# A four-layer block in fp32: the feed-forward's feature reads issued ahead of the following writes, and its normalisation in two halves

## What is computed

```python
x = x + attention_a(layernorm(x))
x = x + ffn(layernorm(x))
x = x + gla(layernorm(x))
x = x + ffn(layernorm(x))
# ffn, with gate_w, up_w [1024, 256], down_w [256, 1024] cubic splines through ~2033 control points each
gate, up = h @ gate_w.T, h @ up_w.T
return (silu(gate) * up) @ down_w.T
```

## Time and profile before

| | us |
|---|---|
| median of 3 runs (lowest, highest) | 847.05 (846.56, 850.43) |
| the profiled execution, its own time | 852.93 |
| span of that execution | 851.2 |

### The profile page before, as it was taken

One profiled execution on the slowest core, in us unless ns is written; L12 is line 12 of the kernel. 1 busy time (PEld: TensorE's weight loads), 2 busy tenths in 40 slices (PEclk: granted clock), 3 DMA queues, 4 the chain that ended last, 5 costly groups with the idle time before them and its releaser, 6 DMA issues.

```text
span 851.2 us, 19705 instructions
## 1 busy us (share of the span) xinstructions
PE 776.4 (91%) x6676; PEld 657.4 (77%) x6676; DVE 629.5 (74%) x1272; ACT 494.8 (58%) x967; POOL 237.0 (28%) x306
## 2 busy tenths in 40 slices
PE   3689999999999999977999989999998879999988
PEld 3567767777777777746988889888888758889887
DVE  7464777777777788836778777789989748887765
ACT  3135545455454555655666657588878746666653
POOL 2942222223232223321000010055656552000000
PEclk9767999999999999977999999999999989999999
DMA  5946566666666654577565651000034125777741
GB/s 183 112 69 88 94 124 100 88 88 88 98 98 94 96 80 78 109 248 262 204 230 218 255 204 45 1 2 2 2 111 168 42 79 202 255 259 272 267 159 50
DMA packets 70960, 111.16 MB, mean 131 GB/s; under 512 B 7061, under 2 KB 27958, under 8 KB 70854
## 3 DMA queue, kind: packets, MB, share of 16 engines
q1 hardware_dynamic: 70896, 110.35, 51.0%
HBM read 41.82 MB, written 42.81 MB: 99 GB/s over the span
## 4 chain that ended last, share of the span: by engine, by line
PE 51%; DVE 14%; issue 9%; DMA 8%; SPq 8%; ACT 6%; POOL 3%; ACTq 0%; DVEq 0%; POOLq 0%
PE bank L414 8%; PE bank L415 6%; PE bank L416 6%; DMA stk<-fx 5%; PE pair_a L878 4%; SPq L586 4%; PE bank L892 4%; PE pair_b L847 4%; DVE inter L1874 3%; DMA fx<-fs 3%; PE pair_a L1166 2%; ACT gact L1457 2%; DVE spline L1952 2%; PE bank L1201 2%; DVE spline L1961 1%
## 5 line engine op out<-in xcount | busy, mean ns | idle before, releaser
L414 PE MATMUL bank<-wd_hi,in_hi 128*128 128x256 f32 x512 | 145.5, 284 | 1.4 <-DVE in_lo L1879 0.9
L416 PE MATMUL bank<-wd_hi,in_lo 128*128 128x256 f32 x512 | 144.9, 283 | 0.0
L415 PE MATMUL bank<-wd_lo,in_hi 128*128 128x256 f32 x512 | 144.5, 282 | 0.0
L668 POOL TENSOR_SCALAR_AFFINE_SELECT prob<-prob 128x512 f32<-128x512 f32 x128 | 82.1, 642 | 217.3 <-ACT prob L1322 217.3
L1322 ACT ACTIVATE prob<-pair_a 128x768 f32<-128x768 f32 x128 | 103.7, 810 | 66.5 <-PE pair_a L878 65.5
L1465 ACT ACTIVATE in_hi<-inter 128x512 fp32r<-128x512 f32 x128 | 80.8, 631 | 105.7 <-DVE inter L1874 100.6
L1703 DVE TENSOR_REDUCE mx<-pair_b 128x6 f32<-128x768 f32 x124 | 118.0, 952 | 26.2 <-PE pair_b L859 25.3
L1879 DVE TENSOR_TENSOR in_lo<-inter,in_hi 128x512 fp32r<-128x512 f32 x128 | 89.1, 696 | 60.5 <-ACT in_hi L1465 59.0
L414 PEld LDWEIGHTS bank<-wd_hi,in_hi 128*128 128x128 f32 x512 | 96.7, 189 | 6.9 <-DVE in_lo L1879 1.7
L415 PEld LDWEIGHTS bank<-wd_lo,in_hi 128*128 128x128 f32 x512 | 96.5, 188 | 4.6
L416 PEld LDWEIGHTS bank<-wd_hi,in_lo 128*128 128x128 f32 x512 | 96.5, 189 | 0.0
(11 more groups left out here) (226 smaller groups left out, 1953.1 us busy)
## 6 DMA issues: line engine op xcount, KB each, us to landing
stk<-fx SPq DMA_DIRECT2D x128, 252.0 KB
stack<-stage SPq DMA_DIRECT2D x192, 128.0 KB, 4.7
fx<-fs SPq DMA_DIRECT2D x32, 512.0 KB, 3.4
fx<-fs SPq DMA_DIRECT2D x32, 256.0 KB, 3.6
fx<-fs SPq DMA_DIRECT2D x16, 504.0 KB
fx<-fs SPq DMA_DIRECT2D x16, 252.0 KB
X<-in_attn_a_x SPq DMA_DIRECT2D x14, 256.0 KB, 5.1
result<-X SPq DMA_DIRECT2D x7, 512.0 KB, 7.9
```

The source lines that it names most:

```text
L414: pe.matmul(dst, l_hi, r_hi, start=first, stop=False)
L415: pe.matmul(dst, l_hi, r_lo, start=False, stop=False)
L416: return pe.matmul(dst, l_lo, r_hi, start=False, stop=last)
L668: pool.affine_select(out=diag, in_=diag, compare_op=ALU.is_ge, fill=0.0, base=0, pattern=[[0, 2], [0, 2], [1, P]], channel_multiplier=-1). ...
```

## The change

Three edits, all in the feed-forward, with the same computation: `read(g+1)` goes ahead of `write_x(g+2)` in SyncE's period; its wait for group g's first up product becomes one for the last up product of group g-1, with a wait for the reads of group g added; and `normalise4(g+3)` is made in two calls of two tiles, behind the gates of blocks 4 and 5.

```diff
@@ sync, ffn
                 def read(g, u):
                     sp.wait_ge(f_.xw, upto(f_.xw, base + g, 64))
                     sp.wait_ge(f_.mw, upto(f_.mw, base + g, 32))
-                    sp.wait_ge(f_.upp, upto(f_.upp, base + g - 1, 1))
+                    sp.wait_ge(f_.upp, upto(f_.upp, base + g - 2, MT))
+                    sp.wait_ge(f_.ld, upto(f_.ld, base + g - 1, 16 * MT))
@@
                 def period(g, u, prev=True, nxt=True, nxt2=True, nxt3=True):
+                    if nxt:
+                        read(g + 1, 1 - u)
                     if nxt2 and prev:
                         write_x(g + 2, u)
-                    if nxt:
-                        read(g + 1, 1 - u)
                     if prev:
                         store(g - 1)
@@ scalar, ffn
-                def normalise4(g):
+                def normalise4(g, tiles=range(2 * TB)):
                     act.wait_ge(f_.mr, upto(f_.mr, base + g, 1))
                     act.wait_ge(f_.xT, upto(f_.xT, base + g - 1, CT))
                     act.sem_inc(passed_act, 1)
-                    for t in range(2 * TB):
+                    for t in tiles:
@@
-                        if m == 5 and nxt3:
-                            normalise4(g + 3)
+                        if m in (4, 5) and nxt3:
+                            normalise4(g + 3, range(TB * (m - 4), TB * (m - 3)))
```

## The result

The changed kernel takes 861.14 us (median of 4 runs, 856.75 to 864.3) where the kernel before, run beside it, takes 847.12 (846.56 to 850.43): a ratio of 1.0134 with an interval of 1.0086 to 1.0183, so it is slower, by about 11 us (the medians alone are 14 us apart, a ratio of 1.0165, which lies in the interval). The forecast was 841.6.

What follows compares the result with a forecast made beforehand. The ScalarE-VectorE exchange (18.76 us a period) was taken as the bound, reads second. Gains of 4.9 us in the first feed-forward and 0.5 in the second, 5.4 in all, took 847.05 to 841.6 us; range 834.5 to 846.5.

Steps and rivals of the forecast that it cites:

- The bound: Feed-forward periods: set by ScalarE and VectorE at 18.76 us, TensorE's own sum being 17.53, with late reads second.
- The exchange: Feed-forward: ScalarE and VectorE alternate high part, low part and gate; 18.76 us from one normalisation to the next.
- The halves: Normalisation as two tiles behind each of blocks 4 and 5: 0.92 us less per period, 17.84; 4.4 per feed-forward.
- rival (c): Normalisation halves push both high parts back and gain nothing; period stays 18.76, total 846.0 us; chance 0.1.
- The ring's shape: SyncE's queue: reads, x, store, moments; the next reads may not be issued until the moments have landed.
- rival (a): Ring does not bind, since reads and writes overlap or seams are hidden; both feed-forwards gain, 836.0 us; chance 0.2.
- The ring's size: From one group's reads to the next's: 19.9 us in the second feed-forward, 18.5 in the first, without the store.
- rival (b): Ring longer than summed, 21.2 us, deciding from about 20.9; reads of group 15 6.0 late; 851.5 us; chance 0.1.
- The ends of my range: Ring values 19.2 and 20.9 us, putting the second feed-forward between 4 us gained and 5 lost.
- The second feed-forward: Ring uses up the 7.5 us lead at 2.1 per group, the 4.4 gain becomes waiting; 0.5 us gained.
- The first feed-forward: Group 7's reads land at 511.5, before it begins near 514; gain 4.4 plus 0.5 before group 6, 4.9 us.
- the prediction's condition for being wrong altogether: TensorE's clock drops below 1.00 in the feed-forward stretches, or the attention or GLA change length.

Runs made afterwards that it cites:

- e5: Kernel before, with only the reads spread over more engines (14 instead of 9): 844.46 us, ratio 0.9961 to the kernel before.
- e4: Changed kernel with the reads spread over more engines (14 instead of 9): 836.43 us, ratio 0.9866 to the kernel before.
- e6: Kernel before with the normalisation in halves and reads on more engines, without the new order: 836.67 us, ratio 0.9848 to the kernel before.
- e1: Kernel before with the normalisation in halves alone: 841.07 us, ratio 0.9915 to the kernel before.
- e9: Changed kernel with `write_x` held until the reads issued ahead of it have landed: 880.67 us, ratio 1.0358 to the kernel before.
- e10: Changed kernel with reads ahead of `write_x` in the first feed-forward alone; halves and new waits kept: 846.67 us, ratio 0.9951 to the kernel before.
- e2: Changed kernel with the normalisation again in one piece, so the new order alone: 860.91 us, ratio 1.0141 to the kernel before.
- e3: Changed kernel with the store issued last, behind the moments' writes: 852.63 us, ratio 1.0016 to the kernel before.
- e7: Changed kernel with reads on more engines and the store issued last: 839.99 us, ratio 0.9873 to the kernel before.

## Why the prediction was wrong, step by step

**The bound, right.** The exchange at 18.76 and TensorE at 17.53 behind it: e5 keeps 18.76, e4 and e6 come to 17.43 to 17.54 between groups 1 and 4. **The halves, right for the period:** predicted 17.84, measured 17.43 between groups 1 and 2, so the exchange was no longer the bound there. The two high parts are not pushed back, as rival (c) had it. Their worth without the order is less than summed: e1's two stages gain 2.2 and 4.2 us, 6.4 where the prediction has 4.4 twice, because the old reads then come late (TensorE waits 0.79, 0.51 and 0.73 us for them before groups 3, 5 and 6). Had the order been left alone, 841.6 would have been close, though not by its own sum: e1 gave 0.9915, 840 us.

**The ring's shape, right.** It binds in the second feed-forward, and its queue is the one that the prediction wrote down. So rival (a) falls.

**The ring's size, the step that failed.** I took 19.9 us in the second feed-forward and 18.5 in the first. The changed kernel has 21.2, 21.5, 20.9, 20.9 and 21.9, mean 21.3, and in the first 19.3 to 20.1, mean 19.7. One term was too small, the reads: 1.7 + 9.6 = 11.3 us in the sum, 13.4 in the changed kernel, 12.9 in e9 with nothing beside them. The writes were summed well, and the store and the moments half a microsecond too long (4.2, measured 3.7). I took the reads from group 8's in GLA, which are the fastest of all sixteen groups': 12.0 us. The kernel before showed more in each group that matters. Its reads of groups 10 to 15 landed after 13.3, 14.0, 13.2, 13.1, 13.0 and 13.3 us; for group 11 two rows give it, the issue and the gate that waits for the landing:

```profile
739.81 6.36 SPq L586 DMA_DIRECT2D stk<-fx  x8
...
753.95 0.49 PE L1111 MATMUL pair_a<-stk,cst 126*128 126x512 f32 x1 [0.83 <-DMA stk<-fx]
```

The landing of 13.3 in the earlier trace rows was in front of me, and I counted it for rival (b) only, explained by a store under way; e9 shows nearly that length with nothing under way. The ends of my range had slips of the same kind: 20.9 adds 1.1 us for what rows 8 give as 1.3, and with 1.3 the range would have reached rival (b); and 19.2 is not the sum less its start of 1.7, which is 18.1. 21.3 - 19.9 = 1.4 us over five rings is 7 us, and that turns the 0.5 us gained of the forecast into a loss.

**The second feed-forward.** Predicted 0.5 gained, measured 9.1 lost. Group 8 starts 5.3 us earlier on the clock of the changed kernel's trace (693.4 against 698.7). The reads of group 15 leave at 816.15, 821.5 on the clock of before, 7.9 later than the 813.6 that they had (predicted: 813.1). The five rings sum to 106.4 where the distances of before sum to 92.5, 13.9 more. Against this stands the lead of 7.5 us, less 1.4 because group 8 itself was longer by that much (18.37 against 16.99), with TensorE's clock at 0.78 on average over 697 to 701 us: 13.9 - 6.1 = 7.8. The landing is 7.8 late, and the last group another 1.3 longer, after the stall. 7.8 + 1.3 = 9.1. Of these, the rings have 13.9 - 7.5 = 6.4 and the slower tail 1.3; group 8's 1.4 is not the change's, as said with the stages. Here the sentence that the last group's tail is the same was wrong as well: the instructions are, but the clock is not.

**The first feed-forward.** Predicted 4.9 gained, measured 0.2 lost. The sum asked only when group 7's reads land; the ring bites earlier and on another engine. The one wait for reads below is group 0's, ahead of the first ring. ScalarE's `high_x` waits for the writes of the group before (waits, 380 to 545 us):

```profile
ACT fs L1448 <- DMA fx<-fs: 5.0, 3, 2.0
...
PE pair_a L1112 <- DMA stk<-fx: 1.5, 1, 1.5
```

I had named this wait for groups 12 and 13 alone. It costs periods of 19.61 and 18.69 (groups 4 and 5) against 17.43 (groups 1 and 2). Then group 6 takes 21.12 in place of 18.92. TensorE stops 1.5 us for VectorE's residual, and its clock falls for some microseconds (the trace has only 1.00 and 0.50 here; what lies between is the mean of a stretch):

```profile
499.00:503.00 4.00, 2.95 (x19) 2.22 (x17) 3.62 (x15) 2.59 (x6) 1.44 (x3) 1.00 0.14 54
503.00:506.00 3.00, 2.52 (x14) 2.45 (x15) 2.30 (x5) 1.37 (x4) 0.72 (x2) 0.77 0.53 171
506.00:510.00 4.00, 4.00 (x25) 3.81 (x25) 2.60 (x5) 3.13 (x7) 0.00 (x0) 0.74 0.58 223
```

So the prediction's condition for being wrong altogether, a clock under 1.00 in these stretches, came true here too. e6, which has no late reads and not the new order, shows the same:

```profile
496.66 0.39 PE L414 MATMUL bank<-wd_hi,in_hi 128*128 128x256 f32 x1 [1.53 <-DVE X L1893]
```

```profile
496.00:500.00 4.00, 3.34 (x14) 3.23 (x15) 3.31 (x6) 2.36 (x6) 0.89 (x2) 0.60 0.87 265
```

It takes back 2.3 us (21.25 against 18.92) of the 5.3 that e6 gains in groups 0 to 5. But e10, whose program is the changed kernel's up to here, has the stall and keeps its clock, and its group 6 takes 20.47:

```profile
501.50 0.36 PE L414 MATMUL bank<-wd_hi,in_hi 128*128 128x256 f32 x1 [1.52 <-DVE X L1888]
```

```profile
501.00:505.00 4.00, 3.50 (x27) 3.35 (x28) 3.30 (x6) 2.36 (x6) 0.73 (x2) 1.00 0.56 184
```

So the two have to be kept apart. The stall is 1.52 or 1.53 us in every profiled run whose reads are ahead or shorter in this feed-forward, e5 without the halves among them: it appears where group 6 no longer starts late, and group 6 is then 1.1 to 1.6 us longer than in the kernel before (20.05 to 20.47 in e2, e3, e5, e9 and e10). The drop of the clock followed in the changed kernel, e4, e6 and e7 (21.1 to 21.3) and not in those five. What decides it stays open.

**Rival (b)** is what happened: its place, its point of decision (a ring of about 20.9) and its sign. It gave 851.5; by the ratio it is 858.4. Its ring of 21.2 was right, and its 6.0 us stand against the 6.4 of the rings. What it lacked is the 1.5 us that it left as gained in the first feed-forward and the 0.2 lost there, the slower tail, and group 8 (9.1 lost in the second where it had 6.0). The last 2 us lie within the interval of the ratio. Its chance of 0.1 was too small, since the forecast was 1.0 us of ring away from its point of decision and the one landing in the rows spoke for it.

## What to carry to other kernels

Before a transfer is moved ahead of others in one queue, write the queue down as a ring, from one issue back to the same issue, with start and landing at each place where an issue waits for something that was issued just before it. If the ring comes within a few per cent of the compute period, take each term from issue to landing in the rounds that the change will touch (here the reads of groups 10 to 15) and not from rates in quiet stretches, because the error is multiplied by the number of rounds. And the first thing to try is to shorten the largest term (here by spreading a transfer over more engines), before its place in the order is changed.

## What was not expected of the hardware

- The same eight reads do not always take the same time with nothing beside them: 12.0 us from issue to landing for group 8's in the kernel before, 12.0 to 12.6 over all runs with reads on nine engines, and 12.85 to 12.97 in the second feed-forward of e9. The rate, 213 against 222 GB/s, accounts for 2.06 MB / 213 - 2.06 MB / 222 = 0.4 of it. What makes up the rest was not found.
- A start of about 1.6 us appears ahead of `write_x` when it is issued into an empty queue (5.6 us from issue to landing in e9) and is hidden when it is queued behind reads (4.0 us from their landing to its own). e9 has this seam more in each ring and pays more for it (23.1 against 21.3 us a ring) than the mixing of reads and writes costs (0.5).
- Going from 9 to 14 engines shortened group 8's reads from 12.0 to 10.4 us only. The rate rose from 222 to 255 and 282 GB/s, where 14/9 would give 345, and SyncE needed 6.65 us to issue the eight in that form in place of 6.2 (e4, from 629.13). Which of the two holds it back was not tried.
- A stall of TensorE of 1.5 us was followed by some microseconds at half clock in four profiled runs and by the full clock in five, with one program in both sets up to that point (the changed kernel and e10). The 5.54 us stall was followed by 0.50, the level of 1.2 GHz, for 3 us, and the 1.8 us stall of the kernel before by 1.00.
